# Two graph layers: the second layer's normalized rows split before they are turned, and turned by DMA transposes

## What is computed

```python
h = relu(layernorm(x))                                   # x: 2048 x 256, adj: 2048 x 2048, 0 or 1
x = x + graph_attention_and_gcn(h, adj, adj)             # layer 1
h = relu(layernorm(x))
# layer 2: attention inside 32 graphs (mask: same graph), adj is added twice to the scores
a = where(mask, (h @ Wq.T + bq) @ (h @ Wk.T + bk).T / 16, 0)
scores = (a + adj + adj) * where(mask, 1, -1e6)
x = x + (softmax(scores) * mask) @ (h @ Wv.T + bv)
```

## Time and profile before

| | us |
|---|---|
| median of 3 runs | 232.29 |
| lowest and highest run | 231.71, 234.67 |
| profiled execution, span from first to last instruction | 231.0 |
| TensorE busy | 222.2 |
| VectorE busy | 183.1 |
| ScalarE busy | 160.1 |
| GpSimd busy | 61.9 |

### The profile page before, as it was taken

One profiled execution on the slowest core, in us unless ns is written; L12 is line 12 of the kernel. 1 busy time (PEld: TensorE's weight loads), 2 busy tenths in 40 slices (PEclk: granted clock), 3 DMA queues, 4 the chain that ended last, 5 costly groups with the idle time before them and its releaser, 6 DMA issues. The chain is left out here.

```text
span 231.0 us, 5379 instructions
## 1 busy us (share of the span) xinstructions
PE 222.2 (96%) x2042; PEld 194.5 (84%) x2042; DVE 183.1 (79%) x452; ACT 160.1 (69%) x308; POOL 61.9 (27%) x115
## 2 busy tenths in 40 slices
PE   7899999999999999999999999999999999999971
PEld 6788888888888888888888888888888889999951
DVE  2589778899995967599984499987699949997783
ACT  3768835899966764995651794666995855888760
POOL 4525860000034000001910001730012043576540
PEclk9799999999999999999999999999999999999999
DMA  6999399007989100752400000000000000012123
GB/s 186 359 374 386 113 332 387 15 0 248 285 316 386 44 3 0 259 177 111 173 12 4 0 0 4 1 3 0 3 0 0 3 0 4 0 50 79 48 72 128
DMA packets 20092, 26.34 MB, mean 114 GB/s; under 512 B 1889, under 2 KB 11873, under 8 KB 20065
## 3 DMA queue, kind: packets, MB, share of 16 engines
q1 hardware_dynamic: 19376, 25.71, 32.2%
q10 hardware_dynamic: 688, 0.27, 0.4%
HBM read 23.88 MB, written 2.10 MB: 112 GB/s over the span
## 5 line engine op out<-in xcount | busy, mean ns | idle before, releaser
L1091 PE MATMUL bank_a<-hd,e_hi 128*128 128x257 f16 x256 | 70.3, 274 | 0.0
L1089 PE MATMUL bank_a<-hd,e_hi 128*128 128x257 f16 x256 | 69.7, 272 | 0.0
L1093 PE MATMUL bank_a<-hd,e_lo 128*128 128x257 f16 x256 | 69.4, 271 | 0.0
L1065 PE MATMUL bank_b<-hb,adjt 128*128 128x259 f16 (+1 forms) x512 | 66.5, 273 | 0.2 <-DVE xb L1661 0.2
L1065 PEld LDWEIGHTS bank_b<-hb,adjt 128*128 128x128 bf16 x512 | 49.3, 97 | 7.5 <-DVE xb L1661 0.5
L704 ACT ACTIVATE e_hi<-e_slot 128x1024 f16<-128x1024 f32 x32 | 33.6, 1051 | 26.7 <-PE bank_a L1093 15.6
L1669 DVE SCALAR_TENSOR_TENSOR e_slot<-e_slot,adjt 128x1024 f32<-128x1024 f32 x32 | 39.0, 1219 | 9.0 <-ACT e_slot L697 9.0
L1675 DVE SCALAR_TENSOR_TENSOR e_lo<-e_slot,e_hi 128x1024 f16<-128x1024 f32 x32 | 39.0, 1219 | 7.3 <-ACT e_hi L704 7.2
L697 ACT ACTIVATE e_slot<-s_row,nbias 128x512 f32<-128x512 f32 x64 | 42.3, 709 | 0.2
L570 POOL TENSOR_TENSOR rs_all<-veb,half_neg 128x2 f32<-128x2 f32 x8 | 6.6, 823 | 88.2 <-DVE veb L1848 88.2
L1089 PEld LDWEIGHTS bank_a<-hd,e_hi 128*128 128x128 f16 x256 | 24.7, 96 | 4.0
(11 more groups left out here) (238 smaller groups left out, 380.8 us busy)
## 6 DMA issues: line engine op xcount, KB each, us to landing
adjt<-in_adj_t SPq DMA_DIRECT2D x16, 1024.0 KB, 9.1
x_all<-in_x SPq DMA_DIRECT2D x4, 512.0 KB, 5.3
out<-adjt SPq DMA_DIRECT2D x16, 128.0 KB, 1.9
adjt<-in_x SPq DMA_DIRECT2D x3, 512.0 KB, 7.4
diag<-in_adj SPq DMA_DIRECT2D x16, 64.0 KB, 3.6
adjt<-in_x SPq DMA_DIRECT2D x2, 256.0 KB, 3.7
e_slot<-in_L_gnn_W_gcnb ACTq DMA_DIRECT2D x1, 256.0 KB, 4.0
e_slot<-in_W_saT SPq DMA_DIRECT2D x1, 256.0 KB, 4.8
```

The costliest lines, as they stand in the source:

```text
L1065: eng.matmul(B[:, r % 2, 0:cols], adjt_block(k, j, r), hb16[:, j, part, 0:cols], start=(j == 0 and part == 0), stop=(j == NT - 1 and part ...
L1089: eng.matmul(A[:, r, 0:D + 1], high, hd16[:, j, 0, 0:D + 1], start=(j == 0), stop=False, skip_group_check=True)
L1091: eng.matmul(A[:, r, 0:D + 1], high, hd16[:, j, 1, 0:D + 1], start=False, stop=False, skip_group_check=True)
L1093: mm = eng.matmul(A[:, r, 0:D + 1], low, hd16[:, j, 0, 0:D + 1], start=False, stop=(j == NT - 1), skip_group_check=True)
```

## The change

The rows of pair p are normalized twice on ScalarE, to f32 (`h1`, now two buffers) and to f16 (`h1n16`, high half). GpSimd subtracts the two to the low half (`h1_low`). SP then issues two DMA transposes a pair (`turn_h1`), one for each tile, of 128 x 512 f16 elements (both halves together), straight into `h1T16`, which now has a place for all eight pairs. The four transposes on TensorE, `h1T_high` and `h1T_low` are gone. The factor H1_SCALE is moved into the variance (`new_moments`). `keys(p)` uses the bank that TURN had and the old one in turns, so it waits for keys_low(p-2) rather than for keys_low(p-1).

The order of the queues is written anew around it. On GpSimd: h1_low(0) and (1) after chunk 2, (2) to (5) ahead of values_low(0); the inverse deviation of tiles 14 and 15 is moved from the loop round p = 4 to ahead of row_sums(0), with h1_low(6) behind it; h1_low(7) stands in the round p = 4 ahead of row_sums(1). On ScalarE: normalize(5) is moved one step earlier, the two tiles of pair 6 from the round p = 4 to before the loop (one ahead of pT_high(0)), those of pair 7 from the round p = 5 to the round p = 4. On VectorE, shifts(14, 16) come earlier in their round. On SP, the transposes stand ahead of all stores. New waits: `normalize_tile` waits for the low half of pair p-2 and for the transposes of pair p-2 to have landed, `keys` and `values` for those of their own pair.

The hunks left out are the constant ROWS = 2, the semaphores' names, the general path (its copies undo H1_SCALE) and the index order in `scores`.

```diff
@@ -198,8 +199,11 @@
 
         room = adjt[:, 0:CHUNK]
-        h1 = room[:, 0:4096].rearrange("p (a t d) -> p a t d", a=8, t=2)
-        h1T16 = room[:, 4096:6144].bitcast(F16).rearrange("p (a k s n) -> p a k s n", a=4, k=KT, s=2)
+        h1 = room[:, 0:1024].rearrange("p (a t d) -> p a t d", a=2, t=2)
+        h1n16 = room[:, 1024:2048].bitcast(F16).rearrange("p (a t s d) -> p a t s d", a=ROWS, t=2, s=2)
+        h1n16_rows = room[:, 1024:2048].bitcast(F16).rearrange("p (a t c) -> p a t c", a=ROWS, t=2)
+        h1T16 = room[:, 2048:6144].bitcast(F16).rearrange("p (a s k n) -> p a s k n", a=NQ, s=2, k=KT)
+        h1T16_blocks = room[:, 2048:6144].bitcast(F16).rearrange("p (a c n) -> p a c n", a=NQ, c=2 * KT)
         gT16 = room[:, 6144:7680].bitcast(F16).rearrange("p (a k s n) -> p a k s n", a=3, k=KT, s=2)
         prob = room[:, 7680:8192].rearrange("p (a n) -> p a n", a=2)
         o_sb = adjt[:, CHUNK:CHUNK + 4096].rearrange("p (a t d) -> p a t d", a=8, t=2)
...
@@ -414,8 +417,14 @@
 
-        TURN, KEYS, VALUES = L[:, 0, :], L[:, 1, :], B[:, :, :]
+        VALUES = B[:, :, :]
         b_norm = L[:, 0, 0:4]
+
+        def keys_bank(p):
+            return L[:, p % 2, :]
+
+        def turned(p):
+            return 16 * 2 * (p // ROWS + 1)
 
         def score_bank(p):
             return A[:, p % 3, :]
...
@@ -493,6 +502,15 @@
 
             refill(2)
             refill(3)
+
+            def turn_h1(p):
+                eng.wait_ge(h1_lo_made, p + 1)
+                for n in range(2):
+                    eng.dma_start_transpose(h1T16_blocks[:, p, :, n * P:(n + 1) * P],
+                                            h1n16_rows[:, p % ROWS, n, :]).then_inc(h1_turned[p % ROWS], 16)
+
+            for p in range(NQ):
+                turn_h1(p)
             for i in range(NT):
                 store(i)
             eng.wait_ge(o_stored, 16 * NT)
...
@@ -588,6 +606,11 @@
                 eng.wait_ge(off_made, 4 * k + 4)
                 eng.tensor_tensor(z_off[:, own], z_one[:, :], off_0[:, :], ALU.add).then_inc(off_ready, 1)
 
+            def h1_low(p):
+                eng.wait_ge(h1_ready, 4 * p + 4)
+                eng.tensor_tensor(h1n16[:, p % ROWS, :, 1, :], h1[:, p % 2, :, :], h1n16[:, p % ROWS, :, 0, :],
+                                  ALU.subtract).then_inc(h1_lo_made, 1)
+
             def values_low(p):
                 eng.wait_ge(v_hi_made, p + 1)
                 eng.tensor_tensor(v16[:, p % 4, :, 1, :], v32[:, p % 2, :, :], v16[:, p % 4, :, 0, :], ALU.subtract) \
...
@@ -621,7 +644,12 @@
                 inv_new_deviation(CT * k - 2, CT * k)
                 if k < LAST:
                     outside(k)
+                if k == LAST - 1:
+                    h1_low(0)
+                    h1_low(1)
             eng.wait_ge(scale_1_made, SCALES)
+            for p in range(2, NQ - 2):
+                h1_low(p)
             values_low(0)
             outside(LAST)
             values_low(1)
...
@@ -632,13 +660,15 @@
 
             eng.wait_ge(x1_ready, NT)
             values_low(2)
+            inv_new_deviation(CT * LAST + 2, NT)
+            h1_low(NQ - 2)
             row_sums(0)
             for p in range(4, NQ - 1):
                 row_bias(p - 2)
                 outer_part(p - 2)
                 values_low(p - 1)
                 if p == 4:
-                    inv_new_deviation(CT * LAST + 2, NT)
+                    h1_low(NQ - 1)
                 row_sums(p - 3)
             values_low(NQ - 2)
             outer_part(NQ - 3)
...
@@ -799,28 +829,29 @@
                     eng.wait_ge(x_again, 16 * NC)
                 eng.activation(words, words, ACT.Copy, bias=0.5).then_inc(half_ready, 1)
 
-            def normalize(p):
+            def normalize_tile(p, n):
+                i = 2 * p + n
                 eng.wait_ge(nb_ready, 2 * p + 2)
                 if p == 0:
 
                     eng.wait_ge(mask_ready, NQ * LAST)
                     eng.wait_ge(b_summed, CT * LAST)
-                for n in range(2):
-                    i = 2 * p + n
-                    eng.activation(h1[:, p, n, :], x1_all[:, i * D:(i + 1) * D], ACT.Relu,
+                wait(eng, h1_lo_made, p - 1)
+                if p >= ROWS:
+                    eng.wait_ge(h1_turned[p % ROWS], turned(p - ROWS))
+                for into in (h1[:, p % 2, n, :], h1n16[:, p % ROWS, n, 0, :]):
+                    eng.activation(into, x1_all[:, i * D:(i + 1) * D], ACT.Relu,
                                    scale=rs_all[:, i:i + 1], bias=nb_all[:, i:i + 1]).then_inc(h1_ready, 1)
 
-            def h1T_high(p):
-                eng.wait_ge(h1_turned, p + 1)
-                wait(eng, s_summed, p - 3)
-                eng.activation(h1T16[:, p % 4, :, 0, :], TURN.rearrange("p (k n) -> p k n", k=KT), ACT.Copy,
-                               scale=H1_SCALE).then_inc(h1T_hi_made, 1)
+            def normalize(p):
+                normalize_tile(p, 0)
+                normalize_tile(p, 1)
 
             def keys_high(p):
                 eng.wait_ge(g_summed, p + 1)
                 wait(eng, s_summed, p - 2)
                 for c in range(KT):
-                    eng.activation(gT16[:, p % 3, c, 0, :], KEYS[:, c * 2 * P:(c + 1) * 2 * P], ACT.Identity,
+                    eng.activation(gT16[:, p % 3, c, 0, :], keys_bank(p)[:, c * 2 * P:(c + 1) * 2 * P], ACT.Identity,
                                    bias=u_s[:, c:c + 1]).then_inc(g_hi_made, 1)
 
             def values_high(p):
...
@@ -905,43 +936,40 @@
                             normalize(2)
                         if q == 2:
                             normalize(3)
-                        if q == 3:
-                            h1T_high(0)
                         if q == 4:
                             normalize(4)
                         if q == 5:
                             keys_high(0)
-                            h1T_high(1)
+                            normalize(5)
                         if q == 6:
-                            normalize(5)
                             values_high(0)
                             keys_high(1)
 
             keep_a(LAST, 0, 2)
-            h1T_high(2)
             tanh_mix(LAST, 0, 2)
             values_high(1)
             keys_high(2)
             keep_a(LAST, 2, CT)
-            h1T_high(3)
             tanh_mix(LAST, 2, CT)
-            h1T_high(4)
             exponents(0, 0)
             exponents(0, 1)
             keys_high(3)
+            normalize_tile(NQ - 2, 0)
             pT_high(0)
             values_high(2)
             exponents(1, 0)
             exponents(1, 1)
+            normalize_tile(NQ - 2, 1)
             for p in range(4, NQ - 1):
                 values_high(p - 1)
-                h1T_high(p + 1)
                 exponents(p - 2, 0)
                 keys_high(p)
                 pT_high(p - 3)
+                if p == 4:
+                    normalize_tile(NQ - 1, 0)
                 exponents(p - 2, 1)
-                if p in (4, 5):
-                    normalize(p + 2)
+                if p == 4:
+                    normalize_tile(NQ - 1, 1)
             values_high(NQ - 2)
             exponents(NQ - 3, 0)
             pT_high(NQ - 4)
...
@@ -1126,26 +1155,16 @@
                 eng.wait_ge(sq_1_made, 4)
                 eng.matmul(L[:, 0, 0:4], ones[:, :], sq_1[:, :], start=True, stop=True).then_inc(norm_1_summed, 1)
 
-            def turn_h1(p):
-                eng.wait_ge(h1_ready, 2 * p + 2)
+            def keys(p):
                 if p == 0:
                     eng.wait_ge(z_kept, NC)
-                wait(eng, h1T_lo_made, p)
+                    eng.wait_ge(w_1_lo_made, 4)
+                eng.wait_ge(h1_turned[p % ROWS], turned(p))
+                wait(eng, g_lo_made, KT * (p - 1))
                 for c in range(KT):
-                    for n in range(2):
-                        mm = eng.transpose(TURN[:, (2 * c + n) * P:(2 * c + n + 1) * P],
-                                           h1[:, p, n, c * P:(c + 1) * P], ident[:, :])
-                mm.then_inc(h1_turned, 1)
-
-            def keys(p):
-                if p == 0:
-                    eng.wait_ge(w_1_lo_made, 4)
-                eng.wait_ge(h1T_lo_made, p + 1)
-                wait(eng, g_lo_made, KT * p)
-                for c in range(KT):
-                    mm = three_products(KEYS[:, c * 2 * P:(c + 1) * 2 * P],
+                    mm = three_products(keys_bank(p)[:, c * 2 * P:(c + 1) * 2 * P],
                                         lambda kk, part: w_qk16[:, kk, part, c * P:(c + 1) * P],
-                                        lambda kk, part: h1T16[:, p % 4, kk, part, :])
+                                        lambda kk, part: h1T16[:, p, part, kk, :])
                 mm.then_inc(g_summed, 1)
 
             def values(p, n):
...
@@ -1153,10 +1172,10 @@
                     if p == 0:
                         eng.wait_ge(b_kept, NT)
                         eng.wait_ge(w_1_lo_made, 4)
```

(32 more changed lines are left out.)

21 lines of the change are left out of this document (10 added, 11 removed).

## The result

The changed kernel takes 241.93 us (median; 240.60 to 243.41) against 233.09 (231.71 to 234.67) for the kernel before on the same chip: ratio 1.0386, 95% interval 1.0306 to 1.0465. It is slower, and by more than the forecast of 238.1 us, but inside the range of 232 to 243, near its upper end. The profiled execution took 243.41 us.

A forecast was written before the change was run, and what follows sets the result against it. TensorE was taken as the bound, the other engines just keeping ahead. Despite 3.5 us of transposes removed, queue delays put gather(3) at 221.25, 5.8 late; 15.5 more gave 236.8 us span, plus 1.3 made 238.1 us, range 232 to 243.

The forecast's parts named there:

- three places: Delays at normalize(4)'s wait for pair 2, GpSimd's order before exponents(2, 0), and the next round; gather(3) 5.8 us late.
- TensorE -3.5: On TensorE, 32 pipelined transposes removed, 0.44 us a pair over eight pairs: 3.5 us less.
- T = 4.15: Pair's DMA transposes, low half to landing: 0.55 us issue plus 3.6 us landing; ends 2.45 and 9.65.
- transposes are the bound: Rival: DMA transposes one after the other, 9.65 us a pair, hold up keys(7); 252 us; chance 0.10.
- First place: Pairs 2 to 5: normalize(4) waits for pair 2's transposes, 183.35 instead of 180.07; keep_a(LAST, 0, 2) 2.55 us late.
- From there to the statistics: VectorE from keep_a(LAST, 0, 2): 1.8 us off, 0.3 added; statistics of the last two tiles finish at 204.0, not 203.0.
- Second place: GpSimd: inverse deviation and h1_low(6) ahead of row_sums(0) put exponents(2, 0) at 207.5, 4.3 us late; gather(1) at 210.0.
- Third place: Next round: h1_low(7) ahead of row_sums(1) and row_bias(3); exponents(3, 0) 6.85 us after exponents(2, 0), at 214.35 instead of 207.72.
- TensorE's idle time: Sign: idle TensorE ahead of gather(0), gather(1) and gather(2), together 9.3 us, 2.4 of it ahead of gather(2).
- the 1.3 us that I added: Beyond the span: median before lay 1.3 us above its profiled span, so 236.8 became 238.1 us.

The follow-up runs named there:

- both_edits: Changed kernel with GpSimd's row_sums(0), row_bias(2) and row_bias(3) ahead of the late pairs' steps, and separate room for f16 rows of pairs 2 and 3; ratio 0.9941 to before.
- one_turn_of_four: Kernel before with 24 of the 32 TensorE transposes left out and nothing else changed, its result not the program's; ratio 0.9899 to before.
- third_place_only: Changed kernel with only h1_low(7) moved behind row_bias(3) on GpSimd; ratio 1.0319 to the kernel before.

## Why the prediction was right, and where it was off

The mechanism and its three places are right: undoing them took the loss away (both_edits). Term by term, each time counted from the origin:

- **TensorE -3.5: right.** one_turn_of_four paid 2.35 of 2.6 us by the ratio, 1.4 in the profiled execution.
- **T = 4.15 from halves to landing: nearly right, by luck, from two wrong parts.** (T is the time from pair 2's halves being ready to both its DMAs having landed.) The first h1_low of 181.82 took 1.61, so the halves of pair 2 were ready at 183.43 and normalize(4) started 4.38 behind. Inside it the issue is dearer and the landing cheaper than I took (0.55 and 3.6). The reason that I gave for 3.6, short pieces, is right: packets under 512 bytes went from 1889 to 10592. But 2.5 us is what they took. The transposes by line (ns of issue min/median/max; then landing):

```profile
L509 SPq DMA_TRANSPOSE adjt<-adjt x16: 1189/1268/2085, 161.0 to 218.8; - x16
...
DMA to landing us min/median/max: 2.4/2.5/4.0
```

  Two issues of some 1.27 and one landing of 2.5 would be 5.0 if nothing overlapped. The rival "transposes are the bound" needed 7.3 us a pair and had no footing: the table of waits of the changed kernel has none of TensorE for a transpose. The Trainium skill (VectorE: DVE Perf Modes, The three transpose paths) gives 1309 ns for one 128x128 block; multiplied by the four blocks of a DMA that was 10.5 us a pair, and the trace does not agree, as a DMA of four blocks lands 2.5 us after its issue.
- **First place: the mis-sized term.** Predicted +3.3 for normalize(4) (183.35 against 180.07); measured 187.81 - 147.85 = 39.96 against 180.07 - 145.41 = 34.66, **+5.3**. The 2.0 too few are: the inverse deviation starts 0.6 later, occupies GpSimd 1.5 instead of 0.7 (+0.8), the first low half takes 1.61 instead of the 1.19 that the sum left for it (179.15 - 177.96, +0.4), T is 0.2 longer. By the rows the 0.6 come from pairs 0 and 1, which I had put on engines with room: behind ScalarE's doubled normalize(0) VectorE's next e_slot operation waits 1.43 instead of 0.45 us, so keep_a of chunk 2 starts 0.3 later, and VectorE's four mixes (L1838) take 2.00 instead of 1.67 us beside h1_low(1). The middle two have, by the rows, one cause; no run changed the neighbour alone. In before this inverse deviation ran while VectorE did h1T_low, which reads PSUM; the change takes h1T_low away, so VectorE's e_slot operation, both inputs in SBUF, moves up beside it. VectorE before, and after:

```profile
177.01 0.68 DVE L1863 SCALAR_TENSOR_TENSOR adjt<-bank_l,adjt 128x512 f16<-128x512 f32 x1
177.61 1.21 DVE L1669 SCALAR_TENSOR_TENSOR e_slot<-e_slot,adjt 128x1024 f32<-128x1024 f32 x1
```

```profile
180.06 1.22 DVE L1680 SCALAR_TENSOR_TENSOR e_slot<-e_slot,adjt 128x1024 f32<-128x1024 f32 x1
181.20 1.22 DVE L1686 SCALAR_TENSOR_TENSOR e_lo<-e_slot,e_hi 128x1024 f16<-128x1024 f32 x1
...
183.44 2.19 DVE L1686 SCALAR_TENSOR_TENSOR e_lo<-e_slot,e_hi 128x1024 f16<-128x1024 f32 x1
```

  The kernel before had the price on show, five us earlier on GpSimd's timeline, where the same instruction met the same neighbour (L1669 at 172.02); I took the 0.71 of the earlier trace rows instead:

```profile
172.23 1.59 POOL L570 TENSOR_TENSOR rs_all<-veb,half_neg 128x2 f32<-128x2 f32 x1 [20.00 <-DVE veb L1848]
```

- **From there to the statistics: right to 0.3.** keep_a followed normalize(4) by 7.58 (predicted 7.8), and the statistics were done 3.3 late (predicted 1.0, with the 2.0 of above 3.0).
- **Second place: right.** From the start of the inverse deviation to exponents(2, 0): 212.26 - 208.84 = 3.42, predicted 207.5 - 204.05 = 3.45. gather(1) 2.57 behind, predicted 2.5.
- **Third place: right in size, incomplete in cause.** exponents(2, 0) to (3, 0) took 6.81, predicted 6.85; from there to the end 22.4, predicted 236.8 - 214.35 = 22.45, so the stores behind the transposes cost nothing that shows. But I had 2.4 of idle TensorE ahead of gather(2), and there is none: the same time went into the lower clock, which the prediction did not have. The size came out right because the second chain, TensorE at the lower clock, happened to be no longer than the queues; that is luck. Had I removed only this place on paper, I would have promised a gain that third_place_only did not have.
- **TensorE's idle time: 9.3 predicted, 7.0 measured** (3.14 + 0.19 + 3.70), plus what the lower clock took, 0.44 x 3.9 + 0.48 x 5.5 = 4.4 us. The sum of 11.4 answers to 8.1 + 3.5 = 11.6. The 3.14 ahead of values(1) were missing from my list, though their cause was in it: keys_high(0) stands behind normalize(4) on ScalarE, VectorE's keys_low(0) waits for it, keep_values(0) stands behind keys_low(0), and values(1) needs its bank. VectorE's keys_low(0):

```profile
190.63 0.88 DVE L1876 SCALAR_TENSOR_TENSOR adjt<-bank_l,u_s,adjt 128x256 f16<-128x256 f32 x2 [3.85 <-ACT adjt L854]
```

So the forecast lay 2.3 us low from the origin (8.1 against 5.8), 2.0 of it in the first place. The profiled span itself lay 4.7 above the predicted 236.8, the rest being the 2.4 ahead of the origin. The median lay 3.8 above the forecast: besides the 2.3, the 1.3 us that I added for what lies beyond the span was 1.9 in the changed kernel's profiled execution (243.41 - 241.5), and 0.9 can't be split by one profile.

## What to carry to other kernels

Work taken off the full engine pays only if the in-order queues of the others keep their small latency-critical steps first: here two subtractions of 1.2 us and an inverse deviation, put ahead of row sums and a 0.7 us row bias, cost more than the 3.5 us that the change took off TensorE, and moving them behind brought back 4.6. A buffer of two, whose next writer waits for a transfer, cost nearly as much (3.6 to 3.9). A price of an instruction is read from the row with the same neighbour, not from the nearest row of the same line. Where a stall also lowers TensorE's clock, queue and clock can be two chains of equal length, and an experiment that removes one of them says little until the other is gone as well.
